# Softmax of an attention: the row maximum is written negated by the reduction itself, and the scale of the scores sits in the copy of the queries

## The reference

```
scale = HD ** (-0.5)                     # 16 heads, HD = 32
x = rmsnorm(layernorm(x), norm_w)
q = (x @ wq.T).reshape(B, L, NH, HD)
k = (memory_tokens @ wk.T).reshape(B, M, NH, HD)
v = (memory_tokens @ wv.T).reshape(B, M, NH, HD)
attn = jnp.einsum('blhd,bmhd->bhlm', q, k) * scale
attn = jnp.where(memory_mask[:, None, None, :], attn, -jnp.inf)
attn = jax.nn.softmax(attn, axis=-1)
out = jnp.einsum('bhlm,bmhd->blhd', attn, v).reshape(B, L, C) @ wo.T
x = x + tanh(g) * sigmoid(x @ wg.T) * out
```

## Time and profile before

| | |
|---|---|
| median of 3 runs | 1218.2 us (1211.73 to 1219.87) |
| the profiled execution's own time | 1216.41 us |
| its span, first to last instruction | 1214.6 us |
| PE busy | 1147.2 us, 94% |
| PEld busy | 986.9 us, 81% |
| DVE busy | 685.2 us, 56% |
| ACT busy | 575.0 us, 47% |
| POOL busy | 437.2 us, 36% |
| mean granted TensorE clock | 0.987 |

### The profile page before, as it was taken

The page is one execution under the profiler, slowest core; times in us unless marked ns, Lnnn a source line. Parts: engine busy times, 40 slices in busy tenths (PEclk is TensorE's granted clock), DMA queues, the critical chain, the costliest instruction groups (busy, mean ns, idle before and its releaser), DMA issues. The chain is left out here.

```text
span 1214.6 us, 24721 instructions
## 1 busy us (share of the span) xinstructions
PE 1147.2 (94%) x7323; PEld 986.9 (81%) x7324; DVE 685.2 (56%) x1411; ACT 575.0 (47%) x1394; POOL 437.2 (36%) x532
## 2 busy tenths in 40 slices
PE   7999999999998789899999999999999999999995
PEld 6887888888875567668777878999999889898994
DVE  6676756756658889637786446432244453424241
ACT  5655655656577678651221116433344443434241
POOL 1014222213327576100067613344434434344443
PEclk9999999999999899899999999999999999999997
DMA  9110000000101031130003218654455675646463
GB/s 336 57 39 1 19 4 19 19 4 19 36 1 27 26 105 35 71 131 1 9 1 125 88 53 258 169 109 70 85 135 147 151 210 88 147 76 151 70 147 70
DMA packets 54939, 100.42 MB, mean 83 GB/s; under 512 B 5638, under 2 KB 22534, under 8 KB 54870
## 3 DMA queue, kind: packets, MB, share of 16 engines
q0 software_dynamic: 15824, 37.76, 16.2%
q1 hardware_dynamic: 39046, 61.78, 15.7%
HBM read 73.04 MB, written 26.48 MB: 82 GB/s over the span
## 5 line engine op out<-in xcount | busy, mean ns | idle before, releaser
L1961 PE MATMUL t_H<-m_W,t_xT 128*128 128x352 f32 x1632 | 280.2, 327 | 4.0 <-DVE t_xT L2040 1.5
L1961 PEld LDWEIGHTS t_H<-m_W,t_xT 128*128 128x128 f32 x1632 | 261.4, 188 | 8.2 <-DVE m_W L2044 3.6
L1929 POOL DMA_INDIRECT out_dram<-t_ys,t_sid x68 | 109.8, 1614 | 218.4 <-ACT t_ys L1996 113.9
L1991 ACT ACTIVATE t_sl<-t_H 128x352 f32<-128x352 f32 x68 | 31.6, 465 | 191.1 <-PE t_H L1961 191.1
L742 ACT ACTIVATE pr<-SC,neg 128x128 f32<-128x128 f32 x256 | 90.8, 377 | 57.5 <-DVE neg L952 56.2
L2080 DVE TENSOR_TENSOR t_hT<-t_TH,t_hT 128x384 fp32r<-128x384 f32 x68 | 37.8, 556 | 97.3 <-ACT t_hT L2024 97.3
L49 PE MATMUL t_Y<-m_W,t_hT 128*128 128x512 f32 (+1 forms) x207 | 88.4, 427 | 4.1 <-issue 3.1
L1996 ACT ACTIVATE t_ys<-t_Y,t_wcol 128x512 f32<-128x512 f32 x69 | 47.5, 688 | 92.5 <-PE t_Y L51 92.5
L2048 DVE TENSOR_TENSOR t_h<-t_H,t_sl 128x352 f32<-128x352 f32 x68 | 35.7, 524 | 86.3 <-ACT t_sl L1991 83.9
L51 PE MATMUL t_Y<-m_W,t_hT 128*128 128x512 f32 (+1 forms) x207 | 82.4, 398 | 0.0
L50 PE MATMUL t_Y<-m_W,t_hT 128*128 128x512 f32 (+1 forms) x207 | 82.3, 397 | 0.0
(11 more groups left out here) (461 smaller groups left out, 3135.3 us busy)
## 6 DMA issues: line engine op xcount, KB each, us to landing
m_raw<-in_L_ffn_w_dram SPq DMA_DIRECT2D x28, 704.0 KB, 5.2
m_raw<-in_L_ffn_w_dram SPq DMA_DIRECT2D x14, 512.0 KB, 4.5
CT<-in_ctx_dram SPq DMA_DIRECT2D x8, 512.0 KB, 3.9
X<-in_x_dram SPq DMA_DIRECT2D x4, 1024.0 KB, 14.5
rows_d<-rows_first SPq DMA_DIRECT2D x16, 256.0 KB, 2.0
out_dram<-X SPq DMA_DIRECT2D x3, 1024.0 KB, 4.3
m_raw<-in_L_ffn_w_dram SPq DMA_DIRECT2D x14, 192.0 KB, 4.9
CT<-in_ctx_dram SPq DMA_DIRECT2D x8, 256.0 KB, 2.6
```

Source lines behind the costliest of these rows:

```text
L1929: pool.indirect_dma_start(out=m["out_rows"][:, :], out_offset=bass.IndirectOffsetOnAxis(ap=sid[:, b:b + 1], axis=0), in_=ys[:, b, :], in_o ...
L1961: x_ = pe.matmul(bk[b % 2][:, 0:I], xT[:, b % 2, jx, k, :], W13[:, jw, k, j, :], start=k == 0 and jx == jw, stop=k == KC - 1 and jx == 1)
```

## The change

The reduction of the scores writes its result negated, straight into `neg`; the tile `mx`, the second DVE instruction with its floor and its scale, and DVE's wait for its own semaphore are gone. DVE's wait for the exponentials of unit t - 2 now stands ahead of the reduction. The scale of the scores is now an immediate scale of ACT's copy of the queries out of PSUM (the keys keep 1.0), and the exponentials lose theirs. The counts on `s_out` are halved to match.

```
@@ tiles
-        mx, neg = sb("mx", [P, 2, HQ]), sb("neg", [P, 2, HQ])
+        neg = sb("neg", [P, 2, HQ])
@@ scalar engine, steps q and k
-                            wait(act, s_out, 8 * (2 * t - 2))
-                            act.activation((qT if kind == "q" else kT)[:, t % 2, s[2], :], src[:, 0:2 * S], ACT.Copy)\
-                                .then_inc(m_act, 1)
+                            wait(act, s_out, HQ * (2 * t - 2))
+                            act.activation((qT if kind == "q" else kT)[:, t % 2, s[2], :], src[:, 0:2 * S], ACT.Copy,
+                                           scale=SCALE0 if kind == "q" else 1.0).then_inc(m_act, 1)
@@ scalar engine, step sm
-                        act.wait_ge(s_out, 2 * t + 2)
+                        act.wait_ge(s_out, t + 1)
...
-                            i = act.activation(pr[:, t % 2, slot, :], SC[t % HQ][:, slot * S:(slot + 1) * S], ACT.Exp, scale=SCALE0,
+                            i = act.activation(pr[:, t % 2, slot, :], SC[t % HQ][:, slot * S:(slot + 1) * S], ACT.Exp,
                                                bias=neg[:, t % 2, slot:slot + 1], accum_out=sums[:, t // HQ % 2, at_:at_ + 1])
@@ vector engine, step sm
                         dve.wait_ge(s_fill, t + 1)
-                        dve.tensor_reduce(mx[:, t % 2, :], bk, AX.X, ALU.max).then_inc(s_out, 1)
-                        dve.wait_ge(s_out, 2 * t + 1)
                         wait(dve, p_exp, t - 1)
-                        dve.tensor_scalar(neg[:, t % 2, :], mx[:, t % 2, :], MASKED / 10, -SCALE0, ALU.max, ALU.mult).then_inc(s_out, 1)
+                        dve.tensor_reduce(neg[:, t % 2, :], bk, AX.X, ALU.max, negate=True).then_inc(s_out, 1)
```

## The result

| | before | after |
|---|---|---|
| median of the runs | 1215.9 us (9 runs) | 1207.1 us (9 runs) |
| the profiled execution's own time | 1216.41 us | 1207.15 us |
| its span | 1214.6 us | 1205.5 us |
| DVE busy | 685.2 us | 671.6 us |
| PE busy | 1147.2 us | 1145.3 us |

The ratio of the times is 0.9931, with a 95% interval of 0.9915 to 0.9947: the changed kernel is 0.7% or 8.4 us faster (0.0069 x 1215.9), 6.4 to 10.3 us. One of the nine runs before took 1610.71 us and is left out of the ratio, as is one of 6373.45 us among the five of the version without the floor further down.

The account below looks back on a forecast made before the run. TensorE was taken as the bound, busy 94% of the span. Relieved waits in the first attention summed to 5.7 us, lowered to 5: 1218.2 - 5 = 1213.2 us, range 1205 to 1221 us.

Parts of the forecast that it names:

- the ledger: TensorE's waits in the first attention, each asked whether L952 stands in its chain; eight items summing to 5.7 us.
- the ceiling of 10.0 us: TensorE's idle time in the 330 us first attention, 330 - 319.96, taken as what a faster partner can win.
- the second rival: "More than the ledger": bubbles shorter than the overlap of pipelined matmuls also go, all 10 us, giving 1208 us; chance 0.12.
- (h): "Issue" waits before projections, two gaps of 1.19 us, one at 153.87 us: 0 to 2.4 us, taken as 1.2.
- (a): L525 at 107.73 us waits for a key copy behind exponentials with a stretched L952: all 0.69 us goes.
- (b): Transposes waiting for exponentials, 1.7 us: two 0.41 us gaps close, a third loses 0.21; gain 1.03 us.
- (e): Waits for spread reciprocals, 2 x 0.39 us, ScalarE's queue unbroken from exponentials delayed by a stretched L952: 0.78 us.
- (f): Waits for the gate, same mechanism as the spread reciprocals: 0.6 us.
- (g): Wait for a key copy at 66.5 us: 0.17 us.
- (c): Waits for transposed copies, 1.4 us: 0.83 us gap at 306.48 us closes, the other loses 0.20; gain 1.03 us.
- Handed on: Instructions behind L952 meet the same GpSimd addition instead; only some 1 us gained, 1217 us; chance 0.25.
- Clock: Clock falls in the second attention land on other work, 2.1 us per stretch; from three on 1219.5 us; chance 0.11.
- Routing: Differently rounded scores or overflow send tokens to other experts; 1240 us with one more pass; chance 0.05.

Follow-up runs that it names:

- the version without the floor: Changed kernel without the floor of 0.5 under the sums (16 small tensor_scalar instructions gone): 0.9917 of the kernel before; repeated 0.9907, median 1203.3 us.
- the spare instruction: Changed kernel plus a tensor_scalar of 128 x 4 behind each reduction, its result read by nobody: ratio 0.9954 to the kernel before.
- the spare reduction: Changed kernel plus a reduction over one element per result behind each reduction, its result read by nobody: ratio 0.9928 to the kernel before.

## Why the prediction was right, and where its sum fell short

**The bound.** The gain of the stage, 9.3 us, is of the size of TensorE's idle time in it, and each large part of it sits at a gap of the ledger or at one beside it. Behind the stage the lead goes up and down for reasons that were not followed. But the ceiling of 10.0 us was read as if idle time were the whole of a stall. It leaves out 0.16 us for each, which the second rival suspected as "bubbles" and the matmuls' start times show.

**What goes.** The stretch beside GpSimd was named as a cost that goes, 8.1 of 21 us of VectorE's queue, and for the time of the kernel it was the larger part: the run with the small instruction as a reduction keeps 7.8 of 9.3 us. The section of the Trainium skill that was named for it (SBUF — State Buffer, Who interferes with whom) says that tensor_reduce never takes the port pair shared with GpSimd; 64 instances within 156 to 159 ns agree.

**What is added, what moves.** All three zeros held: the negation (684 ns both ways), the scale (1.0013 alone), the early wait (0.9999 alone).

**The ledger.** Places and mechanisms were right but for three: the 0.56 us gap at 92.7 us did not shrink (0.55 us after), the gap at 306 us, said to close, kept 0.25 of its 0.83 us, and a third "issue" gap at 60.7 us, taken as 0, gave 0.43 us. The sum was 5.7, lowered to 5; measured were 8.9 in the listed jumps and 9.3 in all. The term that was mis-sized most is (h), the middle between 0 and 2.4 us, where the chip gave the upper end, 2.5. The next is the overlap of matmuls that a gap hides: the eight closed gaps of (a), (b), (e), (f), (g) gave 1.3 us more together than their idle time. The deduction for gaps that open again found nothing up to 350 us, where small steps added up instead; it found its case at 367 us, where the gap before L500 grew and took 0.37 us. (c) was over-sized, 1.03 against 0.57, since a transposed copy of ScalarE still ends the wait there.

**The rivals.** Handed on: the mechanism exists. VectorE's busy time fell by 685.2 - 671.6 = 13.6 us, where 64 x 0.16 + 8.1 = 18.3 us were removed, so by this estimate 4.7 us of stretch went to others. The instructions that grew are L776 (2.2 us in all; three instances take 0.88 us instead of 0.15), the floor under the sums, L956 before and L954 after (1.4 us), and L920 (1.0 us). L915, which the prediction feared for, shrank by 0.9 us. No jump of TensorE's lead up to 350 us shows a cost of it. The rule of the Trainium skill that was set beside it (SBUF — State Buffer, Who interferes with whom: issue order decides, the later one blocks fully) would have made (h) nothing. The rows agree with it for each pair, in that the VectorE instruction ends just behind the addition it met (L952 0.02 us, L915 0.28 us). But between two GpSimd additions in a row the waiting VectorE instruction got its turn, in the rows before, after and with the spare instruction. Clock: in the profiled execution one fall did land on the experts' first matmuls and cost 2.7 us there (see the last section), near the 2.1 us that this rival gave for one. But the second attention lost less to the clock than before: the mean granted clock from 376 to 700 us is 0.97 before and 0.98 after, from 700 to 800 us 1.00 and 0.97. Routing: the same 68 tiles were computed. More than the ledger: the stage gained 9.3 of the 10 us which this rival gave, so it came nearer in size than the forecast, in part for the very reason it named.

**Range and signs.** Neither bound follows from the terms given for it: 1218.2 - 10 - 6.5 = 1201.7 us, not 1205, and 1218.2 + 6.3 = 1224.5 us, not 1221. The measured 1207.1 us lie inside either way. Of the signs for the profile after, two came out short: VectorE's busy time in the whole run fell by 13.6 us, not 15 or more, and the gap near 306 us stayed in part.

## What to carry to other kernels

When a small VectorE instruction is much longer on average than at its minimum, look at what GpSimd does in those places: here, with the 15 stretches of 64 instances gone and the number of instructions as before, 7.8 of the 9.3 us were won. Judge such a change by the waits of the engine that bounds the stage, not by those of the engine that waits most, and measure a stall from start to start of its matmuls. And look past the stretched instruction: whoever comes next in the queue may take its place between two of GpSimd's, which was worth 2.5 us here.

## What the runs showed of the hardware

The granted clock can differ where the schedule does not. The changed kernel and the one with the spare reduction reach the experts' first matmuls within 0.03 us of each other. Four us of each, changed kernel first (us, busy times, then the granted clock, 0.50 and 1.00, the lower and the upper level):

```profile
718.00:722.00 4.00, 3.28 (x11) 3.29 (x12) 0.58 (x1) 0.00 (x0) 2.60 (x7) 0.50 0.78 274
```

```profile
718.00:722.00 4.00, 3.31 (x20) 3.32 (x21) 0.52 (x1) 0.00 (x0) 2.56 (x6) 1.00 0.81 280
```

and the first group of 24 matmuls:

```profile
718.72 6.82 PE L1959 MATMUL t_H<-m_W,t_xT 128*128 128x352 f32 x24 [1.50 <-DVE t_xT L2038]
```

```profile
718.69 4.14 PE L1961 MATMUL t_H<-m_W,t_xT 128*128 128x352 f32 x24 [1.52 <-DVE t_xT L2040]
```

6.82 us against 4.14: a fall of the clock costs 2.7 us here, and the two executions differ by 1205.5 - 1202.7 = 2.8 us in their spans. In the 4 us ahead TensorE was busy for 2.11 us in the one and 2.05 in the other. What made the clock fall in one of them is not settled. These are two different kernels, and the repetition of the changed kernel has the fall at this place again. But one and the same kernel scatters too. The version without the floor reaches the projection at 374.94 us in one execution and at 374.95 in the other, and the experts' first matmuls 2.9 us apart:

```profile
714.82 4.14 PE L1957 MATMUL t_H<-m_W,t_xT 128*128 128x352 f32 x24 [1.52 <-DVE t_xT L2036]
```

```profile
717.75 4.11 PE L1957 MATMUL t_H<-m_W,t_xT 128*128 128x352 f32 x24 [1.53 <-DVE t_xT L2036]
```

In between the mean granted clock is 0.99 in the first and 0.98 in the second (376 to 700 us). How much of the 2.9 us is the clock stays open. A difference of one or two us between kernels can't be read from single spans for that reason, and the stage was measured between its exponentials.
